# Two exponentials by head instead of four in the cross attention, a new static order, and x parts of the up stage on GpSimd

## What is computed

```python
# self attention, then layernorm of the sum
scores = einsum('bqhd,bkhd->bhqk', Q, K) * scale + alibi
out = einsum('bhqk,bkhd->bqhd', softmax(scores, -1), V) @ Wo + bo
# cross attention: the softmax runs over the 112 QUERIES (axis 1), not over the 375 keys
sm = softmax(einsum('nlhd,nshd->nlhs', q, k) / 4, axis=1)
attn = einsum('nlhs,nshd->nlhd', sm, v) @ Wo + bo
# feed forward with 16-bit quantised activations; every act_qdq has ONE scale for the whole tensor
x = act_qdq(x); up = act_qdq(x @ wu.T); gate = act_qdq(x @ wg.T)
gate = act_qdq(gate * fixed_qdq_u16(sigmoid(gate)))
y = act_qdq(gate * up) @ wd.T
```

## Time and profile before

| what | value |
|---|---|
| median of 3 runs | 1305.83 us (1305.64 to 1305.86) |
| profiled execution: its time / its span | 1304.4 us / 1302.6 us |
| TensorE busy | 1140.7 us, 88% of the span |
| ScalarE busy | 1068.6 us, 82% |
| VectorE busy | 1001.3 us, 77% |
| GpSimd busy | 345.5 us, 27% |
| granted TensorE clock, mean of the span | 0.959 |

### The profile page before, as it was taken

One profiled execution on the slowest core, in us unless ns is written; L12 is line 12 of the kernel. 1 busy time (PEld: TensorE's weight loads), 2 busy tenths in 40 slices (PEclk: granted clock), 3 DMA queues, 4 the chain that ended last, 5 costly groups with the idle time before them and its releaser, 6 DMA issues. The chain is left out here.

```text
span 1302.6 us, 28828 instructions
## 1 busy us (share of the span) xinstructions
PE 1140.7 (88%) x8466; PEld 833.1 (64%) x8466; DVE 1001.3 (77%) x2239; ACT 1068.6 (82%) x4083; POOL 345.5 (27%) x431
## 2 busy tenths in 40 slices
PE   1689999999999999999999999999866987778598
PEld 1466666666666666666666666666535976667598
DVE  6268888888888878888788878888853559967688
ACT  1368999998999989999899989999863579968695
POOL 0223334333334333334433333433210000000044
PEclk9899999999999989999999999999976999989799
DMA  5100000100000100000000000010000000000033
GB/s 159 35 16 17 21 20 21 37 21 20 19 20 20 32 26 19 20 19 20 27 29 22 19 20 19 20 30 26 5 7 5 1 1 1 0 1 1 25 102 99
DMA packets 35111, 33.26 MB, mean 26 GB/s; under 512 B 4164, under 2 KB 34748, under 8 KB 35004
## 3 DMA queue, kind: packets, MB, share of 16 engines
q1 hardware_dynamic: 32704, 31.50, 7.9%
q10 hardware_dynamic: 2300, 0.66, 0.3%
HBM read 24.81 MB, written 7.34 MB: 25 GB/s over the span
## 5 line engine op out<-in xcount | busy, mean ns | idle before, releaser
L582 ACT ACTIVATE Px<-score,nmax_h 125x112 f32<-125x112 f32 x1024 | 349.5, 395 | 4.2 <-DVE nmax_h L783 3.1
L582 ACT ACTIVATION_READ_ACCUMULATOR Px<-score,nmax_h 125x1 f32 x1024 | 247.8, 249 | 0.0
L571 ACT ACTIVATE Ps<-score,nmax_s 112x112 f32<-112x112 f32 x512 | 177.1, 435 | 6.0 <-DVE nmax_s L790 6.0
L571 ACT ACTIVATION_READ_ACCUMULATOR Ps<-score,nmax_s 112x1 f32 x512 | 147.7, 289 | 0.0
L783 DVE TENSOR_REDUCE nmax_h<-score 125x8 f32<-125x896 f32 x128 | 138.5, 1082 | 7.2 <-PE score L1028 6.3
L502 POOL TENSOR_TENSOR Qbd_hi<-Qx_hi,mask 128x448 fp32r<-128x448 f32 x64 | 59.7, 933 | 293.8 <-DVE Qx_lo L799 293.8
L1028 PE MATMUL score<-Qbd_hi,KxT_hi 64*125 64x448 f32 x384 | 91.6, 472 | 35.9 <-POOL Qbd_lo L502 26.6
L523 POOL TENSOR_TENSOR rstd<-vare,half 112x1 f32<-112x1 f32 x64 | 35.1, 548 | 320.9 <-DVE vare L875 320.9
L1120 PE MATMUL outX<-Px,Vn 125*32 125x224 f32 x1536 | 109.4, 373 | 5.0 <-DVE Vn L766 5.0
L623 ACT ACTIVATE PsT<-work 112x448 f32<-112x448 f32 x128 | 74.6, 583 | 33.1 <-PE work L1155 32.4
L1608 PE MATMUL gbank<-xq_hi,w_upT_hi 128*128 128x448 f32 x192 | 73.8, 385 | 27.8 <-ACT xq_lo L1402 27.8
(11 more groups left out here) (244 smaller groups left out, 3500.0 us busy)
## 6 DMA issues: line engine op xcount, KB each, us to landing
ctx_in<-in_ctx SPq DMA_DIRECT2D x32, 375.0 KB
x_in<-in_x SPq DMA_DIRECT2D x32, 112.0 KB, 2.1
x_scratch<-x SPq DMA_DIRECT2D x32, 112.0 KB, 1.9
x2T_all<-x_scratch SPq DMA_DIRECT2D x32, 112.0 KB, 2.1
out<-x2T_all SPq DMA_DIRECT2D x32, 112.0 KB, 1.9
raw_w_up<-in_w_up SPq DMA_DIRECT2D x1, 768.0 KB, 5.8
raw_w_down<-in_w_down SPq DMA_DIRECT2D x1, 768.0 KB, 7.4
raw_w_gate<-in_w_gate SPq DMA_DIRECT2D x1, 768.0 KB, 9.5
```

Of the source, the lines that this page charges most:

```text
L571: ins = act.activation(Ps[:, g, :], score[slot][0:L, h // QUAD, (h % QUAD) * L:(h % QUAD + 1) * L], ACT.Exp, bias=nmax_s[:, g:g + 1], accu ...
L582: ins = act.activation(Px[u % 2][:, h, :], score[SLOT_OF[f"C{u}"]][0:C, h // QUAD, (h % QUAD) * L:(h % QUAD + 1) * L], ACT.Exp, bias=maxim ...
```

## The change

`BY_HEAD` shrinks from units 1, 3, 4, 5 to units 1 and 4, so units 3 and 5 become shifted. The order of all five `step` functions, `WORK_USES` and `SLOT_USES` are written anew. In the up stage the parts of x of groups 1 to 7 are converted by GpSimd (`up_parts`), those of group 0 still by ScalarE.

```diff
-BY_HEAD = (1, 3, 4, 5)
+BY_HEAD = (1, 4)
...
 SLOT_USES = (
-    (("C5", 1), ("C1", 2), ("C2", 2), ("C4", 2)),
-    (("C0", 2), ("S0", 4), ("C3", 2), ("S1", 4)),
+    (("C2", 3), ("C4", 3), ("C5", 3), ("C1", 4)),
+    (("S0", 5), ("C3", 3), ("S1", 5), ("C0", 4)),
 )
...
+            def up_parts(g, p):
+
+                pool.wait_ge(product, g * 2 + (NH - 2))
+                pool.tensor_copy(xh[p][0][:], xpart(x2T_all, g, 0))
+                pool.tensor_copy(xh[p][1][:], xpart(x2T_all, g, 1)).then_inc(up_parts_done, 1)
+
+            def up_step(g, p, last):
+                if not last:
+                    up_parts(g + 1, 1 - p)
+
+            over_groups(pool, up_step)
...
                 if last:
                     parts(HIDDEN, 0, 0)
-                else:
-                    parts(UP, g + 1, 1 - p)
                 sigmoid(g, 1)
...
-                pe.wait_ge(x_parts, g + (stage * NG + 1))
+                if stage == UP and not (isinstance(g, int) and g == 0):
+                    pe.wait_ge(up_parts_done, g)
+                else:
+                    pe.wait_ge(x_parts, g + {GATE: 1, UP: NG + 1, HIDDEN: NG + 2}[stage])
```

More of the change, by code:

```diff
@@ L724, in step @@
                     exp_self(n4, 1)
+                if n3:
+                    hi_keys_cross(n3, 1)
+                if n2:
+                    copy_max(n2, 5)
+                if n4:
+                    hi_context(n4, 0)
+                if n2:
+                    exp_shifted(n2, 5)
+                if n4:
+                    copy_probs(n4, 2)
+                    copy_probs(n4, 3)
+                    even_self(n4, 0)
+                if n3:
+                    copy_max(n3, 0)
+                if n4:
+                    hi_context(n4, 1)
+                if n3:
+                    exp_shifted(n3, 0)
+                if n2:
+                    even_cross(n2)
+                if n1:
+                    copy_x2T(n1)
+                if n4:
+                    even_self(n4, 1)
+                if n3:
+                    exp_by_head(n3, 1)
+                if n4:
+                    hi_keys_cross(n4, 0)
+                if n5:
+                    exp_self(n5, 0)
+                if n3:
+                    copy_max(n3, 2)
             iterations(act, step)
@@ L923, in step @@
                 if n4:
[L924 to L928, removed]
+                    pick_self(n4, 0)
                 if n2:
@@ L931, in step @@
                 if n4:
-                    lo_context(n4, 0)
+                    divide_self(n4, 0)
+                    lo_context(n4, 1)
                 if n3:
                     max_cross(n3, 1)
+                    sum_cross(n3, 0)
                 if n4:
-                    lo_context(n4, 1)
                     pick_self(n4, 1)
+                if n3:
+                    reciprocal_cross(n3, 0)
+                if n4:
                     divide_self(n4, 1)
+                if n2:
+                    pick_cross(n2)
+                if n3:
+                    normalise_values(n3, 0)
                 if n5:
@@ L1198, in step @@
+                if n3:
+                    cross_values(n3, 1)
+                    transpose_max(n3, 3)
+                if n5:
+                    transpose_probs(n5, 1)
+                if n6:
+                    transpose_x(n6)
                 if n3:
-                    transpose_ctx(n3, 1)
-                    self_values(n3, 1)
+                    cross_scores(n3, 4)
+                    shift(n3, 3)
+                if n6:
+                    project_T(n6, "Ks", w["aWk"], xT, "xT")
@@ L1242, in _ @@
+                if n5:
+                    transpose_probs(n5, 3)
+                    self_values(n5, 0)
+                    transpose_ctx(n5, 1)
+                if n4:
+                    transpose_max(n4, 0)
+                    cross_scores(n4, 1)
+                    shift(n4, 0)
+                if n3:
+                    cross_values(n3, 5)
             iterations(pe, step)
```

250 lines of the change are left out of this document (106 added, 144 removed).

## The result

The changed kernel takes 1270.53 us (median of 4 runs, 1270.1 to 1272.59), the kernel before 1305.74 us (median of 4, 1303.99 to 1305.86). The ratio is 0.9737, 95% interval 0.972 to 0.9753: 2.6% faster. The direction of the prediction was right. Its size was not: it forecast 1293 us with a range that began at 1280, so -12.6 us where -35 came. The profiled execution took 1270.9 us.

The account below looks back on a forecast made before the run. TensorE (26.2 us) and ScalarE (25.6 us) were taken to bound the attention step together. From 1304.4 us, attention steps -2.6, filling and draining -4 and up stage -6 gave 1291.8, as median 1293 us; range 1280 to 1318.

Parts of the forecast that it names:

- TensorE's term: Attention step: two more units' transposes and shifts add 0.62 us a unit, 1.24 us a step, to TensorE.
- the floor of 27.5 us: Attention step: TensorE's work of 26.25 + 1.24 us, the lowest possible step, with no waits and none at the jump.
- The term that "speaks against the change": Attention step: TensorE's added 1.24 us, since the change unloads the second engine and loads the first.
- The sentence on the jump: ScalarE's loop jump, 0.6 us between the two kinds of step, can lie in a pause, with 4.8 us to spare.
- The stretches at 1.2 GHz: Attention loop: the granted clock falling more often to its lower level would make the prediction wrong; no size given.
- The wait for Qbd: TensorE's 0.9 to 1.0 us wait before unit 0's scores; forecast gone, with Qbd about 0.5 us early.
- the layout: New attention order laid out by row distances: no matmul has to wait, high keys drained 0.1 to 0.3 us early.
- The list of what would make the prediction wrong: Signs: mean step 28.4 us or more, TensorE distances well over 0.2 and 0.4, lower clock oftener, copies over 2 us.
- The up stage: Parts of x moved to GpSimd make VectorE the bound there: -6 us, bounds -9.6 and +1.
- the cheap price of the copy: Up stage: a GpSimd copy costs by elements read, 0.93 us for 896, against 1.86 us by elements written.
- The rule that the prediction cited: Two-SBUF-input VectorE instructions contend with GpSimd reading SBUF, first started keeps the pair; reductions never contend, so only `glu` is hit.
- Filling and draining: Ends of the attention pipeline: a pipeline shorter by 6 to 7 us, counted in part as -4 us, bounds -8 and +3.

Follow-up runs that it names:

- e5: Changed kernel with each transpose of maxima done twice, four more TensorE transposes a step; 1280.02 us, ratio 0.9796.
- e3: Changed kernel with units 3 and 5 by head again, without their transposes, shifts and sums, in the new order; 1376.26 us, ratio 1.0541.
- e9c: e3 with ScalarE's loop jump one operation earlier, ahead of unit 2's copy of maxima, same order of operations; 1330.05 us, ratio 1.0191.
- e2: Kernel before with only the x parts of up groups 1 to 7 moved to GpSimd; 1297.76 us, ratio 0.9943.
- e6: Kernel before with each transpose of maxima done three times, four more a step; 1312.38 us, ratio 1.0041.
- e12: Kernel before with ScalarE's loop jump four operations earlier, same order of operations; 1314.38 us, ratio 1.0068.
- e1: Changed kernel with the up stage's x parts of all groups back on ScalarE; 1277.64 us, ratio 0.9781.
- e4: Kernel before in its old order, with units 3 and 5 shifted and their added operations put in by hand; 1362.18 us, ratio 1.0426.
- e7: Changed kernel with VectorE's low keys of half 1 moved ahead of the cross block's norm; 1262.63 us, ratio 0.9658.
- e8: Changed kernel with GpSimd's up-stage copies held until glu is done; 1269.58 us, ratio 0.9717.
- e10c: Changed kernel with both low keys ahead of the norm and GpSimd's copies held until after glu; 1260.41 us, ratio 0.9661.
- e11c: The changed kernel run again unchanged, beside e10c on one chip; 1271.86 us, ratio 0.9745.

## Why the prediction was right in direction and wrong in size

**TensorE's term (1.24 us a step) was sized twice too large.** It is about 0.6 us by the rows of the changed kernel. TensorE's whole work in a step grew by still less, from 26.2 to 26.6 us by the steps without their waits (26.2 to 26.5 by the windows), where the prediction had 27.5. The prediction read one transpose and one shift as distances from start to start and rounded them up. The transpose was read in front of a score product, and the shift at 0.37 us, which holds the passage to the next kind of matmul, paid by any last product of a unit. The marginal costs are 0.08 us (e5, mean of four places) to 0.16 for the transpose and 0.19 to 0.20 for the shift. With 0.6 in its place the prediction's own sum gives 26.25 + 0.6 + 0.25 = 27.1 us, and 27.00 was measured. That this comes so close is in part luck: it is made of 26.6 us of work and 0.4 of waits, where the mended sum has 26.85 and 0.25. So 0.65 us of the step's miss of 0.75 is this term, some 16 us over 25 steps. The whole miss of the span, 20.9 us, is this term, 2 us net of the other work and waits in the loop, 6.7 us of stretches at 1.2 GHz, less 4 us in which the terms outside the loop gave less than forecast. It also set the floor of 27.5 us on which the range stood. The term that "speaks against the change" was the one that failed.

**The sentence on the jump failed in its reason.** It said that the 0.6 us of the jump "can lie in a pause", given ScalarE's free time. The 0.6 us did go, and the sum was right to leave them out, but ScalarE's free time was not the reason: e3 and e9c have the same work and the same packets, and the place of the jump alone makes a pause of 4.8 to 6.1 us a turn or of at most 1.1. In the changed kernel the packets went with the mix, 910 instructions fewer on ScalarE. Whether its jump would lie in a pause if they had stayed wasn't tried.

**The stretches at 1.2 GHz were not in the sum.** The prediction named more of them as a danger, and they vanished: 6.7 us. The 25 steps have 4 of them in before, e2 and e6, 6 in e12, 14 in e3, and none in the changed kernel, e1, e4, e5, e7, e8, e9c, e10c and e11c. They occur only in kernels with a pause of ScalarE at every jump. All four of before begin 1.2 to 2.3 us after such a pause has ended, the six of e12 3.0 to 4.3 us after. From e3 to e9c, where only the place of the jump moves, 14 become none. So TensorE's standing still behind that pause is a cause of them. Which of TensorE's pauses bring one on, and why only some of the turns have one, stays open. e4, whose TensorE is busy 46.5 of 50 us, as little as that of e12 with 46.6, has none; its single waits are 1.1 us at most, those of e12 up to 1.8.

**What held.** ScalarE fell by 2.8 us a step (25.6 to 42.21/50 x 27.00 = 22.8), forecast 2.9. VectorE rose to 46.31/50 x 27.00 = 25.0 us, forecast 24.8. That both engines bound the old step is borne out by e6, whose step took a third of what TensorE was given. The wait for Qbd went. What waits remained are 0.4 us a step, for VectorE as said, where 0.25 was allowed: the layout had found the high keys of that bank in time, and did not name the low ones behind the norm. The list of what would make the prediction wrong had only signs of a slower result: distances "well over" 0.2 and 0.4 us, and not under them.

**The up stage held nearly in full.** -5.4 against -6 us; the cheap price of the copy, with 0.93 us, was the right one; only `glu` was hit, by 0.37 to 0.75 us where 0.4 was taken (six groups, 3.8 us in all, against 2.8); `glu` by `glu` the groups with copies are 9.2 to 9.5 us apart, forecast 9.1 to 9.3 (the last 8.8). The rule that the prediction cited, of the Trainium skill, SBUF — State Buffer, section Who interferes with whom, is borne out by e8: with the copies kept out of `glu`, both take their own time and no reduction is ever longer. It also holds for the other side, which the prediction left out: a copy that starts during `glu` waits for it (2.26 in place of 0.94 us), harmless here, as it is needed a group later.

**Filling and draining** came to -1.5 and not -4 us: filling gained 7.8, a little more than the 6 to 7 us that were worked out, but draining lost 6.3. The prediction said that the gain counts "in part", and not that the end steps could give back nearly all.

## What to carry to other kernels

A small matmul put among others costs what the next start moves back, and this must be read at a place where the same neighbours stand with and without it; a start-to-start distance beside another kind charges it with costs that are there anyway, and where this term sets the floor of the forecast, the whole range stands too high (here by 0.65 us a step). Where every second step of an unrolled loop is longer, look at each engine's idle time without a releaser at the jump and at the packets of its instruction queue: a shorter list can be worth more than the work it saves, and a jump that is exposed can be moved without changing the order of anything. A static order is made for one mix of operations: either half of this change alone made the kernel 4 to 5% slower, and the new order with the old mix was still 1.9% slower with its jump moved.

## What the runs showed of the hardware

- ScalarE's loop with four units by head is loaded again at each turn, about 5 packets of 8 KB; with two units by head it is not. The pause at the jump is 0.64 us (before), 2.13 us (e12) or 5.24 us (e3), or hidden but for 1.0 to 1.1 us at three of ten jumps (e9c), with the same 79 packets. It ends 1.65 to 1.95 us after a packet has started.
- A stretch of 3.4 us at 1.2 GHz lengthened a step of the kernel before by 1.2 to 1.4 us, one of 6.8 us by 2.8 us; in e12, where TensorE stands still longer, four of the six steps with one take 29.95 to 30.02 us and two 29.58 and 29.62, against 29.47 to 29.65 without: 0 to 0.5 us more.
- A conversion of 128x896 from 16-bit integers on GpSimd takes 0.93 us, the same as on ScalarE, and up to 2.26 us beside a two-input operation on VectorE.
